# Four buffers per store, a folded scaling and leading transposes in a two-layer attention kernel

## What is computed

```python
def gnn(inp, adj, W_w, W_b, a):                       # first block
    h = einsum('bnf,of->bno', inp, W_w) + W_b; h[:, 0] = 0
    mask = adj[1:, :] > 0
    neigh = einsum('ji,bjf->bif', mask, h[:, :N-1])
    s = einsum('bif,fi->bi', h, a[:F]) + einsum('bif,fi->bi', neigh, a[F:]); s[:, 0] = 0
    hp = s[:, :, None] * h.sum(1)[:, None, :]
    return where(hp >= 0, hp, 0.01 * hp)
def gat(h, mask, b):                                  # attention of h with itself
    scores = where(mask, einsum('...nd,...md->...nm', h, h), -1e16)
    return einsum('...nm,...md->...nd', softmax(scores), h) + b
def two_layers(x, graph, Wh, bh, Wo, bo, gamma, beta):
    mask = graph + eye(N) > 0
    z  = leaky_relu(concat_heads(gat(einsum('bnc,hdc->bhnd', x, Wh), mask, bh)), 0.2)   # layer 1
    z2 = leaky_relu(gat(einsum('bnk,dk->bnd', z, Wo), mask, bo), 0.2)                   # layer 2
    return layernorm(z2) * gamma + beta
x = layernorm(x + gnn(x, adj, ...)); x = layernorm(x + two_layers(x, adj, ...))
```

## Time and profile before

| | us |
|---|---|
| median of 3 runs | 3260.2 |
| lowest, highest | 3257.19, 3266.08 |
| the profiled execution | 3251.58 |
| its span in the trace | 3249.8 |

### The profile page before, as it was taken

One profiled execution on the slowest core, in us unless ns is written; L12 is line 12 of the kernel. 1 busy time (PEld: TensorE's weight loads), 2 busy tenths in 40 slices (PEclk: granted clock), 3 DMA queues, 4 the chain that ended last, 5 costly groups with the idle time before them and its releaser, 6 DMA issues. The chain is left out here.

```text
span 3249.8 us, 124603 instructions
## 1 busy us (share of the span) xinstructions
PE 2940.8 (90%) x49399; PEld 2167.3 (67%) x49399; DVE 2726.6 (84%) x5616; ACT 2311.3 (71%) x2766; POOL 2535.8 (78%) x1431
## 2 busy tenths in 40 slices
PE   5856699999999999999999999999998699999980
PEld 3425577777777777777777777777766666666660
DVE  6764588888888888888888888888876489999997
ACT  2146577777777777777777777777775467777776
POOL 1136589999999999999999999999987078888880
PEclk8989999999999999999999999999999999999995
DMA  5207889899989998898899989998987768988872
GB/s 208 73 1 263 231 154 155 156 169 165 161 157 167 164 164 156 163 167 165 157 163 169 162 155 163 172 163 157 160 139 181 222 144 153 156 154 154 147 132 88
DMA packets 1442506, 514.17 MB, mean 158 GB/s; under 512 B 1359054, under 2 KB 1416844, under 8 KB 1439884
## 3 DMA queue, kind: packets, MB, share of 16 engines
q1 hardware_dynamic: 1442060, 507.32, 80.3%
HBM read 105.27 MB, written 66.06 MB: 53 GB/s over the span
## 5 line engine op out<-in xcount | busy, mean ns | idle before, releaser
L547 POOL TENSOR_TENSOR low<-probs 128x1024 f16<-128x1024 f32 x1280 | 2397.0, 1895 | 408.1 <-ACT probs L820 319.2
L820 ACT ACTIVATE probs<-scores,shifted_max 128x2048 f32<-128x2048 f32 x640 | 1282.5, 2004 | 244.6 <-DVE shifted_max L1033 243.0
L686 PE MATMUL ps<-operands 128*128 128x512 f16 x2560 | 973.4, 380 | 4.8 <-DMA v_parts<-h_d 2.5
L687 PE MATMUL ps<-operands 128*128 128x512 f16 x2560 | 972.8, 380 | 0.0
L1028 DVE CUSTOM_DVE_ANT_0 scores<-ps,mask,neg_max 128x1024 f32<-128x1024 f32 x640 | 821.8, 1284 | 131.4 <-issue 83.8
L695 PEld LDWEIGHTS ps<-ident,probs 128*128 128x128 bf16 x10240 | 648.2, 98 | 411.3 <-issue 246.0
L846 ACT COPY probsT<-ps 128x1024 bf16<-128x1024 bf16 x640 | 647.5, 1012 | 352.4 <-PE ps L695 352.3
L1028 DVE CUSTOM_DVE_ANT_0 scores<-ps,mask 128x1024 f32<-128x1024 f32 x640 | 781.6, 1221 | 119.9 <-PE ps L687 106.7
L695 PE MATMUL ps<-ident,probs 128*128 128x128 bf16 x10240 | 780.8, 219 | 48.6 <-DVE probsT L1040 43.2
L706 PE MATMUL ps<-v_parts,probsT 128*128 128x64 f16 x10240 | 684.8, 193 | 0.0
L705 PE MATMUL ps<-v_parts,probsT 128*128 128x64 f16 x10240 | 684.4, 193 | 0.0
(11 more groups left out here) (142 smaller groups left out, 1840.7 us busy)
## 6 DMA issues: line engine op xcount, KB each, us to landing
operands<-hT_d SPq DMA_DIRECT2D x40, 512.0 KB, 4.1
operands<-hT_d SPq DMA_DIRECT2D x80, 256.0 KB, 4.2
v_parts<-h_d SPq DMA_DIRECT2D x40, 512.0 KB, 4.4
probsT<-low SPq DMA_TRANSPOSE x1280, 3.5
z_d<-outs SPq DMA_DIRECT2D x38, 512.0 KB, 3.7
scores<-in_adj SPq DMA_DIRECT2D x16, 1024.0 KB, 4.8
h_d<-probs SPq DMA_DIRECT2D x32, 512.0 KB, 3.5
hT_d<-probs SPq DMA_DIRECT2D x32, 512.0 KB, 2.8
```

What stands on the lines that cost most here:

```text
L547: pool.tensor_tensor(low[:, u, w], probs[:, u, w], high[:, u, w], ALU.subtract).then_inc(sem(f"low{half}"), 1)
L686: pe.matmul(ps[:, b, :], hi_lo[:, p, t * P:(t + 1) * P], hi_lo[:, p, w], start=True, stop=False)
L687: scored = pe.matmul(ps[:, b, :], hi_lo[:, p, t * P:(t + 1) * P], lo_hi[:, p, w], start=False, stop=True)
L820: act.activation(probs[:, 1 - u, :], scores[:, 1 - u, :], ACT.Exp, bias=shifted_max[:, 1 - u:2 - u], scale=-1.0, accum_out=row_sum[:, held ...
```

## The change

Three edits.

1. In the operand stage `h_parts` and `hT_parts` take w = k % 4. `h_parts(0..3)` now fill `probs`, and `hT_parts(0..3)` lie in `probsT`. The loops `units` become `quads`, with one batch (four units) as the body. The semaphores `h_stored` and `hT_stored` become four each; a unit waits for the store of unit k - 4. In layer 1 the second and third tile's exponential wait for the stores of h of the last four units, and the first copies into `probsT` for those of hT.
2. In `normalize` the scaling L1086 and the addition L1088 become one `scalar_tensor_tensor` (total * -1/64 + bank); in `centre_x` so do L1147 and L1149.
3. TensorE runs 74 transposes of the fp16 identity into PSUM bank 7 after `pool_const` and ahead of its wait for the weights.

```diff
-        def h_parts(u):
-            return stage16(probs, u, 0, H * G * P)
-
-        def hT_parts(u):
-            return stage16(probs, u, H * G * P, H * G * P)
+        def h_parts(w):
+            return stage16(probs, w // 2, w % 2 * H * G * P, H * G * P)
+
+        def hT_parts(w):
+
+            return probsT[:, w // 2, w % 2].rearrange("p k n -> p (k n)")
...
-        def stores(k, u):
+        def stores(k, w):
+
+            return (k - w) * 4
...
             def serve_units(b):
...
+                for w in range(4):
+                    store_h(b, w)
+                    store_hT(b, w)
...
-            for u in range(2):
-                sp.wait_ge(sem(f"h_stored{u}"), 8 * (UNITS - NT // G))
-                sp.wait_ge(sem(f"hT_stored{u}"), 8 * (UNITS - NT // G))
+            for w in range(4):
+                sp.wait_ge(sem(f"h_stored{w}"), 4 * (UNITS - 4))
+                sp.wait_ge(sem(f"hT_stored{w}"), 4 * (UNITS - 4))
             for k in range(OPERAND_DMAS):
                 load_part(0, 0, k)
             serve_units(B - 1)
             for k in range(OPERAND_DMAS):
                 load_part(1, 1, k)
...
             pe.wait_ge(sem("pool_const"), 7)
+            for _ in range(74):
+                pe.transpose(banks16(7, 1)[:, 0:P], ident_h[:, :], ident_h[:, :])
             pe.wait_ge(sem("weights_loaded"), 16 * 9)
...
-            units(pe, p1_step)
-            turn_h(UNITS - 1, 1)
+            quads(pe, p1_step)
+            turn_h(UNITS - 1, 3)
...
-            def p1_step(k, u):
+            def p1_step(k, w, b):
+                u = w % 2
                 act.wait_ge(sem("p1_h"), k + 1)
 
                 since(act, sem("p1_hT"), k - 1)
-                since(act, sem(f"h_stored{u}"), stores(k, u))
-                act.copy(by_tiles(h_parts(u), 0), products(u)).then_inc(sem("p1_hi"), 1)
+                since(act, sem(f"h_stored{w}"), stores(k, w))
+                act.copy(by_tiles(h_parts(w), 0), products(u)).then_inc(sem("p1_hi"), 1)
...
                     if isinstance(i, int) and i == 0 and t <= 2:
-                        act.wait_ge(sem(f"h_stored{t - 1}"), 8 * UNITS)
-                        act.wait_ge(sem(f"hT_stored{t - 1}"), 8 * UNITS)
+                        act.wait_ge(sem(f"h_stored{2 * t - 2}"), 4 * UNITS)
+                        act.wait_ge(sem(f"h_stored{2 * t - 1}"), 4 * UNITS)
...
                 if back(2):
+                    if isinstance(i, int) and i == 0 and t <= 3:
+                        dve.wait_ge(sem(f"hT_stored{t - 2}"), 4 * UNITS)
...
-                    dve.tensor_reduce(mean, by_tile(group_bank(k)), AX.X, ALU.add).then_inc(sem("n_sum"), 1)
+                    dve.tensor_reduce(total, by_tile(group_bank(k)), AX.X, ALU.add).then_inc(sem("n_sum"), 1)
                     dve.wait_ge(sem("n_sum"), n)
-                    dve.tensor_scalar(mean, mean, -1.0 / D, None, ALU.mult).then_inc(sem("n_mean"), 1)
-                    dve.wait_ge(sem("n_mean"), n)
-                    dve.tensor_tensor(by_tile(group_bank(k)), by_tile(group_bank(k)), over_four(mean), ALU.add).then_inc(sem("n_centred"), 1)
+                    dve.scalar_tensor_tensor(by_tile(group_bank(k)), over_four(total), -1.0 / D, by_tile(group_bank(k)), ALU.mult, ALU.add).then_inc(sem("n_centred"), 1)
...
-                dve.tensor_scalar(ln_of(3, b), ln_of(3, b), -1.0 / D, None, ALU.mult).then_inc(sem("n_mean2"), 1)
-                once(dve, "mean2", b + 1)
-                dve.tensor_tensor(by_tile(x1), by_tile(x1), over_features(ln_of(3, b)), ALU.add).then_inc(sem("n_centred2"), 1)
+                dve.scalar_tensor_tensor(by_tile(x1), over_features(ln_of(3, b)), -1.0 / D, by_tile(x1), ALU.mult, ALU.add).then_inc(sem("n_centred2"), 1)
```

More of the change, by code:

```diff
@@ L372, in _ @@
                 load_part(1, 1, k)
-            for u in range(2):
-                sp.wait_ge(sem(f"h_stored{u}"), 8 * UNITS)
-                sp.wait_ge(sem(f"hT_stored{u}"), 8 * UNITS)
+            for w in range(4):
+                sp.wait_ge(sem(f"h_stored{w}"), 4 * UNITS)
+                sp.wait_ge(sem(f"hT_stored{w}"), 4 * UNITS)
             def store_z(i, p, base=0):
@@ L788, in copy_xT, with copy_hT, p1_step @@
                 act.copy(xT_parts(u), banks16(u, 1)[:, 0:G * P]).then_inc(sem("p1_xT_copied"), 1)
[L790 removed]
+            def copy_hT(k, w):
                 act.wait_ge(sem("p1_hT"), k + 1)
[L792 to L795 removed]
+                since(act, sem(f"hT_stored{w}"), stores(k, w))
+                act.copy(hT_parts(w)[:, 0:2 * G * P], banks16(6, 1)).then_inc(sem("p1_hT_a"), 1)
+            def p1_step(k, w, b):
+                u = w % 2
                 act.wait_ge(sem("p1_h"), k + 1)
                 since(act, sem("p1_hT"), k - 1)
[L799 to L800 removed]
+                since(act, sem(f"h_stored{w}"), stores(k, w))
+                act.copy(by_tiles(h_parts(w), 0), products(u)).then_inc(sem("p1_hi"), 1)
                 if within(k + 1):
@@ L803, in p1_step @@
                 if within(k - 1):
-                    copy_hT(k - 1, 1 - u)
+                    copy_hT(k - 1, (w + 3) % 4)
             copy_xT(0, 0)
-            units(act, p1_step)
-            copy_hT(UNITS - 1, 1)
+            quads(act, p1_step)
+            copy_hT(UNITS - 1, 3)
             def tile_step(g, i, t, p, back, second):
@@ L999, in _, with copy_hT, p1_step @@
                 variance(i)
-            def copy_hT(k, u):
+            def copy_hT(k, w):
                 dve.wait_ge(sem("p1_hT"), k + 1)
-                since(dve, sem(f"hT_stored{u}"), stores(k, u))
-                dve.tensor_copy(hT_parts(u)[:, 2 * G * P:4 * G * P], banks16(7, 1)).then_inc(sem("p1_hT_b"), 1)
-            def p1_step(k, u):
+                since(dve, sem(f"hT_stored{w}"), stores(k, w))
+                dve.tensor_copy(hT_parts(w)[:, 2 * G * P:4 * G * P], banks16(7, 1)).then_inc(sem("p1_hT_b"), 1)
+            def p1_step(k, w, b):
+                u = w % 2
                 dve.wait_ge(sem("p1_hi"), k + 1)
-                dve.tensor_tensor(by_tiles(h_parts(u), 1), products(u), by_tiles(h_parts(u), 0), ALU.subtract).then_inc(sem("p1_lo"), 1)
+                dve.tensor_tensor(by_tiles(h_parts(w), 1), products(u), by_tiles(h_parts(w), 0), ALU.subtract).then_inc(sem("p1_lo"), 1)
                 if within(k - 1):
-                    copy_hT(k - 1, 1 - u)
-            units(dve, p1_step)
-            copy_hT(UNITS - 1, 1)
+                    copy_hT(k - 1, (w + 3) % 4)
+            quads(dve, p1_step)
+            copy_hT(UNITS - 1, 3)
             def tile_step(g, i, t, p, back, second):
```

45 lines of the change are left out of this document (17 added, 28 removed).

## The result

| kernel | median us | lowest to highest | profiled execution | its span |
|---|---|---|---|---|
| before (4 runs) | 3261.29 | 3257.19 to 3266.08 | 3251.58 | 3249.8 |
| changed (4 runs) | 3215.39 | 3214.32 to 3216.66 | 3214.32 | 3212.5 |

The ratio is 0.9863, with a 95% interval from 0.985 to 0.9875: 46 us faster, where 63 were forecast. By the two profiled executions it is 37 us, since that of before was a quick one of its kind.

The account below looks back on a forecast made before the run. Bound by TensorE's work in layer 1, VectorE in layer 2, store latency in the operand stage. Gains 34 + 2 + 27 + 0 = 63 us take the median 3260.2 to 3197 us; range 3185 to 3216.

Parts of the forecast that it names:

- Part 1: Layer 2 and last stretch: folding the scaling into the centring gains 34 us and 2 us.
- lower bound of 22: Layer 2: gain of 22 us if VectorE-TensorE coupling through PSUM brings back 0.4 us of waiting per group.
- rival (b): Layer 2: VectorE and TensorE too closely balanced, TensorE still waits 0.5 us per group; 3211 us, chance 0.08.
- The last stretch's 2 us: Last stretch, where VectorE's work is the chain: dropping L1147, run eight times, gains 2 us, possibly 1.
- Part 2: Operand stage: four buffers end the store wait, 2.80 us per unit instead of 3.65; gain 27 us, range 15 to 32.
- Unit 3: Operand stage: with its buffer free, this unit's copy comes 2.1 us earlier.
- The end of the stage: Operand stage's last units up to layer 1's first tiles: 4 us gained, between 2 and 7.
- Rival (a): Operand stage: DMA cannot hold its burst rate, 3.2 us per unit, gain only 15 us; 3209 us, chance 0.14.
- Part 3: Kernel start: 74 transposes end by about 11.2 us, before the weights arrive; gain 0, from -0.5 to +2.5 us.
- I am wrong if layer 1 changes its pace: Layer 1: its pace of 4.08 us per tile stays, since no edit touches it; a change would refute the forecast.

Follow-up runs that it names:

- the split: Changed kernel with the 512 KB load of v_parts cut into two of 256 KB, at tiles 6 and 7: 3196.76 us, ratio 0.9808.
- pad_to_206: Changed kernel without the 74 transposes, with 360 long-met waits on TensorE ahead of layer 1's loop: 3207.79 us, ratio 0.9841.
- a_again: The changed kernel itself run once more, giving a second trace: 3213.98 us, ratio 0.9849.
- b_again: The kernel before run once more, unchanged, for a second trace: 3254.37 us.
- no_warm: Changed kernel without the 74 transposes: 3264.4 us, ratio 1.0004 against the kernel before.

## Why the prediction was wrong

**The bound.** Layer 1 at TensorE's work, layer 2 at VectorE's, the operand stage at the stores' latency: right for the two stages that were changed, each by the rows of after.

**Part 1, in mechanism right, in size a quarter too large.** The fused instruction took the 0.43 us forecast. A typical group of layer 2 lasts 16.49 us by the exponentials' starts, where before it lasted 17.63 and 16.45 was taken: the 1.15 us per group came. The missing 9 us (25.2 for 34) stand in single groups. Some 4 are stalls of the ninth tile, which come through now that TensorE is the bound: the split takes 4.4 us off layer 2 (532.1 to 527.7) here and 4.3 at the place of pad_to_206. Another 4 stand in the one group behind the end of layer 2's loop: 22.3 us (22.2 in a_again), where before had 19.5 (21.0 in b_again) and should have lost 1.1 as well; what makes it long was not taken apart. So TensorE did 94.5 tiles in 400 us, by its 378 matmuls of L689, and not 97. The lower bound of 22 named a coupling of VectorE and TensorE, not this, and rival (b)'s 0.5 us in every group is not there. The last stretch's 2 us did not show: `centre_x` got quicker as forecast, L1152's 1.22 us being followed by the fused L1154 at once,

```profile
3138.63 0.69 DVE L1049 COPY probsT<-ps 128x1024 bf16<-128x1024 bf16 x1 [7.46 <-PE ps L698]
...
3157.11 1.22 DVE L1152 TENSOR_REDUCE scratch<-xs 128x16 f32<-128x1024 f32 x1
3158.36 1.23 DVE L1154 SCALAR_TENSOR_TENSOR xs<-scratch,xs 128x1024 f32<-128x1024 f32 x1
```

but VectorE's last copy of layer 2 waited 7.46 us there, before 4.86, and the piece from the last exponential to the end grew by 1.3.

**Part 2, right step by step.** Forecast 2.80 us per unit, measured 2.69: 91.3 - 67.4 = 23.9 us where 21.2 stood. Unit 3 came 1.2 us later than before and not 2.1 earlier, as the stage itself began 2.7 us late in this execution (L804 first at 248.11; in a_again the first exponential was 4.6 us earlier than in the first profile). The end of the stage gave 4.5 us at the first exponential and 1.9 at the fifth, which comes after the loads of instance 1, where the sum had 4. One pair of executions is a rough measure of this: over all traces the fifth exponential stood at 390.9 to 396.0 us with two buffers and at 364.6 to 369.1 with four, 26.5 us apart on average, and 27 were forecast. Rival (a) is refuted: 381 GB/s held for 74 us. The Trainium skill (DMA: Bandwidth & Descriptors, "Specifications") gives a limit of about 358 GB/s to HBM per core; the stores of this kernel, which runs on one core, went past it, so it is no limit here.

**Part 3 and layer 1, the wrong step.** The sum puts part 3 at nothing ("Cost nothing; the cover is 2.4 us") and has no term for layer 1, "since no edit touches it". The first is true of what the transposes do, at 3.08 to 8.64 us (11.2 was forecast, at the price of transposes at a lower clock; and there was no clock to raise for the weights' transposes, which the kernel before ran at a granted clock of 1.00 from 13 to 15 us). It leaves out that they are 148 instructions of code (147 by the count, as one wait merges with another), and that part 2's longer code (`quads`) is 357 more, ahead of a loop that jumps back 13 times. Alone, 74 transposes cost 26 us; in the changed kernel they are worth 46 us by the ratios (no_warm's 1.0004 against 0.9863), since they take the loop's end from 57 to 204 of its last block. The second is false by the runs: layer 1 took 14 us more in the profiled pair. None of the rivals had a way by which code that is off the path changes a later stage. The text gave the sign for it, "I am wrong if layer 1 changes its pace", and thought it idle.

**The sum.** In the profiled executions' terms 62.6 us were forecast and 37.3 came: 14 lost in layer 1, 9 short in layer 2, 3 at the end, and the lead at the first exponential was met (27.3 for 27). Of the 14, 2.7 are the lead shrinking up to the fifth exponential, and 11.7 are the stall of the ninth tile, which the split removes. Layer 1's edge had no share in it, and that is luck: parts 2 and 3 together happen to leave the loop in a cheap place, where parts 1 and 2 without part 3 would have brought nothing at all. So it is luck too that the median of 3215.4 us lies just inside the range's end of 3216: neither the price of the place nor the stall was in the sum or its bounds. Of the 25 us by which the profiled pair fell short the medians gave 9 back: the kernel before lies 10 us above its profiled execution and the changed kernel 1, where the sum had put 9 for both. That leaves the 17 us that the gain fell short. Three runs of before spread by 9 us, and they said then that a profiled execution can be off by as much.

## What to carry to other kernels

A loop of thousands of instructions on one engine has a price at its jump that depends on what stands ahead of it in the code. So a change that adds or removes instructions ahead of such a loop should be timed at two or three paddings (waits that are long met will do) before it is called good or bad: here an edit that gained nearly 29 us in its own stage looked, alone, like a loss of 31. In the profile, look for waits on "issue" whose count is that of the loop's passes, and for one packet more per pass in the queue of instruction transfers.

And when parts are timed alone, they need not add up: time them together, and look at the stage that no edit touches first.

## What was not expected of the hardware

- TensorE's jump back over 4707 instructions cost 0.3 us where the loop's end lay 131 to 237 instructions into a block of 256, 1.9 at 103, and 3.4 to 4.8 at 5 to 57 (edge less the 4.08 us of a tile). Leaving the loop cost 3 to 5 us at 204 to 237, and nothing at 131 and below (7.1 to 9.0 us for that tile, against 4.2).
- 74 fp16 transposes of 128 x 128 from rest took 5.56 us, 0.075 each, at a granted clock of 1.00, where sixteen at a granted clock of 0.58 took 0.11 each.
- The DMA queues moved 381 GB/s over 74 us of stores, at a share of 1.08 of the 16 engines' time.
- A 512 KB load issued ahead of two transposing DMAs cost TensorE 1.7 us at one tile, and its waits for these DMAs 14.4 us in 1900; with the load in two halves, a tile apart, the waits were 4.2 us, and 1.0 at the place of pad_to_206.
